# A two-layer decoder on one core: VectorE takes two of the four state rows of each step of the first scan's multiply by C

## The reference, cut to what matters

```python
def step(h, inp):
    dt_t, B_t, C_t, x_t = inp
    dA = jnp.exp(dt_t[:, :, None] * A[None])
    h = dA * h + (dt_t * x_t)[:, :, None] * B_t[:, None, :]
    y = jnp.einsum('bdn,bn->bd', h, C_t)
    return (h, y)
```

## Time and profile before

| | us |
|---|---|
| median of 3 runs | 3955.61 (3954.16 to 3958.93) |
| the profiled execution | 3953.2 |
| its span | 3951.4 |
| first scan, first decays to last sum (from the trace) | about 98 to 438 |
| VectorE busy over the span | 3177.0 (80%) |
| TensorE busy over the span | 3507.1 (89%) |
| GpSimd busy over the span | 1339.6 (34%) |

### The profile page before, as it was taken

The page is one execution under the profiler, slowest core; times in us unless marked ns, Lnnn a source line. Parts: engine busy times, 40 slices in busy tenths (PEclk is TensorE's granted clock), DMA queues, the critical chain, the costliest instruction groups (busy, mean ns, idle before and its releaser), DMA issues. The chain is left out here.

```text
span 3951.4 us, 41155 instructions
## 1 busy us (share of the span) xinstructions
PE 3507.1 (89%) x15310; PEld 1468.3 (37%) x15310; DVE 3177.0 (80%) x2733; ACT 1607.1 (41%) x2189; POOL 1339.6 (34%) x493
## 2 busy tenths in 40 slices
PE   5777779998999979998999989988999989976998
PEld 1222243334333443334333443334333443323444
DVE  5999569787999869887999869897999869895333
ACT  5666343214655353214655343214655343212001
POOL 3454304352344304352344304352344304351000
PEclk9788899989899999989899989999999989987999
DMA  6678402122233402122233302122233302110322
GB/s 230 244 277 299 172 15 74 58 74 71 88 106 97 136 22 72 60 72 72 88 105 98 131 27 72 57 75 72 88 105 98 133 25 72 58 45 11 104 96 72
DMA packets 105429, 382.92 MB, mean 97 GB/s; under 512 B 14224, under 2 KB 27920, under 8 KB 102800
## 3 DMA queue, kind: packets, MB, share of 16 engines
q1 hardware_dynamic: 85792, 346.50, 25.5%
q10 hardware_dynamic: 19440, 33.79, 3.1%
HBM read 290.80 MB, written 64.32 MB: 90 GB/s over the span
## 5 line engine op out<-in xcount | busy, mean ns | idle before, releaser
L300 PE MATMUL ps<-r,ring 128*128 128x512 bf16 (+1 forms) x2040 | 782.6, 384 | 0.0
L297 PE MATMUL ps<-xr,ring 128*128 128x512 bf16 x1568 | 613.1, 391 | 0.3 <-PEq L1822 0.3
L301 PE MATMUL ps<-xr,ring 128*128 128x512 bf16 x1568 | 610.6, 389 | 0.0
L297 PE MATMUL ps<-r,ring 128*128 128x512 bf16 (+3 forms) x1384 | 547.8, 397 | 55.2 <-DVE xc L1107 17.8
L301 PE MATMUL ps<-r,ring 128*128 128x512 bf16 (+3 forms) x1384 | 546.9, 396 | 0.0
L1159 POOL TENSOR_TENSOR hh<-hh,bc 128x2048 f32<-128x2048 f32 x72 | 334.7, 4649 | 520.9 <-DVE hh L1069 520.9
L1159 POOL TENSOR_TENSOR bc<-bc 128x2048 f32<-128x2048 f32 x64 | 304.2, 4752 | 344.7 <-DVE bc L1069 344.7
L1159 POOL TENSOR_TENSOR r<-r,bc 128x2048 f32<-128x2048 f32 x56 | 260.9, 4659 | 298.5 <-DVE r L1069 298.5
L1069 DVE TENSOR_TENSOR_SCAN hh<-da,hh 128x2048 f32<-128x2048 f32 x72 | 325.6, 4522 | 1.2
L1110 DVE TENSOR_TENSOR xc<-xc,ps 128x512 f32<-128x512 f32 x176 | 119.3, 678 | 225.0 <-PE ps L301 225.0
L1069 DVE TENSOR_TENSOR_SCAN bc<-da,bc 128x2048 f32<-128x2048 f32 x64 | 296.1, 4627 | 0.5
(11 more groups left out here) (269 smaller groups left out, 6519.5 us busy)
## 6 DMA issues: line engine op xcount, KB each, us to landing
ring<-wsplit SPq DMA_DIRECT2D x216, 768.0 KB, 4.2
r<-wstream SPq DMA_DIRECT2D x54, 768.0 KB, 6.9
ring<-wsplit SPq DMA_DIRECT2D x76, 512.0 KB, 4.0
wsplit<-ring SPq DMA_DIRECT2D x38, 768.0 KB, 4.5
da<-r ACTq DMA_DIRECT2D x360, 63.9 KB, 2.0
wsplit<-r SPq DMA_DIRECT2D x14, 768.0 KB, 4.6
r<-wstream SPq DMA_DIRECT2D x19, 512.0 KB, 6.2
r<-xT SPq DMA_DIRECT2D x7, 1024.0 KB, 6.3
```

The costliest lines, as they stand in the source:

```text
L297: mm = pe.matmul(out, w_hi, x_hi, start=start, stop=False)
L300: pe.matmul(out, w_hi, x_lo, start=False, stop=False)
L301: return pe.matmul(out, w_lo, x_hi, start=False, stop=stop)
```

## The change

In a call without feed-forward tiles (`halved`), GpSimd multiplies rows 0 and 1 of each quartet, and VectorE rows 2 and 3, right after `inputs(step+1)`. VectorE's part tells a new semaphore `own_read`, and `reduce_quad` waits for both. All other calls keep their instructions.

```diff
+        own_read, halved = sem("own_read"), not tiles
...
             def reduce_quad(j):
                 pe.wait_ge(read, 4 * j + 4)
+                if halved:
+                    pe.wait_ge(own_read, 4 * j + 4)
...
                 if step + 1 < blocks:
                     inputs(step + 1)
+                if halved and step < blocks:
+                    dve.wait_ge(scanned, step + 1)
+                    own = quartet(step)[:, GRP // 2:GRP, :]
+                    dve.tensor_tensor(own, own, k.out_rows[:, GRP // 2:GRP, :], ALU.mult).then_inc(own_read, 1)
                 if LAG <= step < pieces + LAG:
                     take_down(step - LAG)
...
             for s in range(blocks):
                 pool.wait_ge(scanned, s + 1)
-                pool.tensor_tensor(quartet(s), quartet(s), k.out_rows, ALU.mult).then_inc(read, 1)
+                rows = slice(0, GRP // 2 if halved else GRP)
+                pool.tensor_tensor(quartet(s)[:, rows, :], quartet(s)[:, rows, :], k.out_rows[:, rows, :], ALU.mult).then_inc(read, 1)
```

## The result

| | kernel before | changed kernel |
|---|---|---|
| median us (7 runs each) | 3957.98 | 3945.04 (3942.21 to 3951.57) |
| ratio, 95% interval | | 0.997 (0.9959 to 0.9981) |
| profiled execution, its span | 3953.2, 3951.4 | 3942.21, 3940.4 |
| start of the last sum's take-out in the first scan | 437.42 | 426.19 |

The changed kernel is 0.3% faster, 12.9 us by the medians; forecast were 9.9 us and 3945.7. The level lies closer to the forecast than the gain does because the median of the kernel before is 3957.98 over seven runs, where it was 3955.61 over the first three: that is luck. Of the 11.0 us between the two spans, the first scan holds 11.2; what follows it takes 3514.0 us before and 3514.2 after.

A forecast was written before the change was run, and what follows sets the result against it. VectorE taking turns with GpSimd, beside a loop of TensorE, ScalarE and weight loads, was taken as the bound. The walk's 8.7 us plus 1.2 at the end gave 9.9, from median 3955.6 to 3945.7; range 3932 to 3956.

The forecast's parts named there:

- The turns: First scan: VectorE and GpSimd alternate whole instructions when both operands are in SBUF; GpSimd's turn falls from 4.5 to 2.24 us.
- rival "slower": First scan: no turn shrinks and each own half adds 1.14 us in some 24 steps; 27 us slower, 3983; chance 0.08.
- The step sums: Steps set by VectorE: 8.88 to 7.9 us without a low part, 10.3 to 9.3 with one; gain 0.35 with `finish_y`.
- The rule of the Trainium skill: Elementwise work belongs on VectorE; by it alone each step gains 2.24 less 1.14 us, some 35 us in all.
- The walk: Through the first scan, counting gains that reach places where TensorE or ScalarE waits for VectorE; sum 9.9 us.
- the second and third stretch: First scan to 206.66, then to 256.29: TensorE idles and follows VectorE; gain reaches 3.0, then 6.3 us.
- the first stretch: First scan, start to 188.96: TensorE's and ScalarE's own chain fixes `inputs` twice; gain 0.
- the whole gain arrives: First scan: step gains and saved lost turns arrive if TensorE's chain also gets faster; 18 to 28 us, 3932; chance 0.14.
- the loop: First scan: a second loop of TensorE, ScalarE and weight loads beside VectorE's; where it sets the step, shorter VectorE steps gain nothing.
- Taken back by the loop: First scan: TensorE, ScalarE and weight loads bind also in steps given to VectorE; 0 to 6 us gain, 3952; chance 0.21.

The follow-up runs named there:

- the added work without the shorter turn: Against the kernel before: GpSimd still multiplies all four rows, and VectorE does an extra 128x1024 multiply on other data into an unused tile; 3987.28 us, ratio 1.0079.
- the run with the half first: Against the changed kernel: VectorE's half moved from behind `inputs` to right behind the scan, ahead of the low part; 3968.01 us, 23 us slower.
- the short rests: Float32 matmul of each weight rest left out, in both kernels: 3946.46 us on the kernel before, 3914.79 on the changed kernel; the pair differs by 31.7.

## Why the prediction was right

**The turns.** Right in both directions: all scans at 4.4 us, line 1066 at 0.68, and the added work without the shorter turn 31.6 us slower. The rival "slower" rested on turns that don't shrink. GpSimd's half took 2.35 us and not 2.24, which lets it end 0.1 later; VectorE's half pays for it with 0.2 us in steps without a low part.

**The step sums.** 7.86 us for 7.9; 9.32 for 9.3 (135.74 to 145.06 in the changed kernel's trace); 8.51 for 8.5 with `finish_y` (232.22 to 240.73). `finish_y` is uncovered, as argued.

**The rule of the Trainium skill** (GPSIMD Engine Reference, Performance versus the Vector engine) that elementwise work belongs on VectorE would have given 35 us here, and by the same rule all four rows should be better still. The runs say 12.9 for two rows and 5.9 slower for four, against the kernel before: what counts here is how long the two engines' turns are together, and what else VectorE has to do beside GpSimd's. What the trace showed of the turns (6.60 us for a scan of 4.41, 5.97 for a GpSimd multiply of 4.52) agrees with the Trainium skill, SBUF — State Buffer, Who interferes with whom: an exclusive lock for a whole instruction. That the waiting engine gets the turn ahead of the holder's next instruction is from the run with the half first (3.90 us at 303.60).

**The walk.** The gains at the places where the path passes between the engines, from starts in the two traces:

| place in the kernel before | forecast | measured |
|---|---|---|
| `inputs` after 188.96 | 0 | 3.5 |
| spread, 206.66 | 3.0 | 6.5 |
| spread, 256.29 | 6.3 | 9.8 |
| `inputs`, 285.75 | 6.3 | 8.1 |
| `inputs`, 349.28 | 8.3 | 9.7 |
| scan behind line 1063, 384.46 | 8.7 | 11.4 |
| last take-out, 437.42 | 9.9 | 11.2 |

In the second and third stretch 3.0 and 3.3 us were gained, as forecast, and behind the last scan 1.1 for 1.2. The other stretches were off, in both directions. In the first stretch I had TensorE's chain run through from the start and gave it nothing, but the spread at 134.78 had idled 1.89 us for line 1063, and the rests behind it now start at 134.06 and not at 135.84: 1.8 us. The remaining 1.7 are matmuls that ran less long at TensorE's lower clock (pairs of 1.91 and 1.46 us from 148.84 before, 1.37 and 1.02 after; of 1.91 and 1.42 from 179.64 before, 1.83 and 1.02 after). The same thing went the other way from 256.29 to 285.75, where I kept the gain at 6.3 and 1.6 us were lost. The rests of the changed kernel there:

```profile
250.72 1.91 PE L228 MATMUL ps<-r,squares_sb 128*128 128x512 f32 x2
252.85 1.37 PE L228 MATMUL ps<-r,squares_sb 128*128 128x512 f32 x2
...
266.08 1.58 PE L228 MATMUL ps<-r,squares_sb 128*128 128x512 f32 x2
```

and those of the kernel before:

```profile
260.59 1.26 PE L228 MATMUL ps<-r,squares_sb 128*128 128x512 f32 x2
261.90 1.02 PE L228 MATMUL ps<-r,squares_sb 128*128 128x512 f32 x2
...
274.76 1.02 PE L228 MATMUL ps<-r,squares_sb 128*128 128x512 f32 x2
```

A pair takes 1.02 us where the granted clock is 1.00 of full speed (2.4 GHz; 271.0 to 272.5 in the changed kernel) and 1.91 to 2.08 where it is 0.50 (1.2 GHz; 248.5 to 252.5). TensorE had idled 1.99 us ahead of this stretch in the changed kernel (4.30 before), so shorter idling did not bring a higher clock, against what I put down for the rival "the whole gain arrives". What sets the moment of the rise stays open.

From 349.28 to 384.46 the gain grew by 1.7 for 0.4: in the kernel before, ScalarE's high part of 357.12 had waited 1.40 us for its load, and in the changed kernel there is no such wait there.

```profile
357.12 1.48 ACT L260 ACTIVATE ring<-r 128x1536 bf16<-128x1536 f32 x1 [1.40 <-DMA r<-wstream]
```

Behind 384.46 I let TensorE follow VectorE with its whole gain. It had idled only 2.37 us there; in the changed kernel its own chain sets that spread (374.52 for 384.68, a gain of 10.2), and `inputs` at 411.94 gains 10.2, not the 11.4 reached before.

So the 9.9 came near the 11.2 partly by luck. The terms that I had too small (3.5 in the first stretch, 1.3 by the late load) and too large (1.6 by the clock, 0.4 on the way to 349.28, 1.4 at the end) nearly cancel.

**The rivals.** "The whole gain arrives" (18 to 28 us) is refuted for this kernel; that the loop holds it back is confirmed by the short rests, where 31.7 us arrive. "Taken back by the loop" was the right mechanism at a smaller size: VectorE's waits for TensorE and ScalarE rose from 17.1 to 31.2 us, where I had looked for 20 or more in `inputs` alone; that part came to 18.9, and the late low parts took the 12.3.

## What to carry to other kernels

A busy share can hold waiting. Where VectorE's operation with two operands in SBUF is longer than elsewhere, look for GpSimd beside it, and count the pair as one queue; dividing GpSimd's work paid here, where VectorE has an operation without such a need (an operand in PSUM) to run beside it. Then walk the path through the places where another engine idles for the sped-up one: what is gained arrives there, at most as far as that engine had idled, and what is queued behind a wait adds to the path. Expect such a walk to be off by a us or two in a stretch, as here by TensorE's clock and a late load. Before an operation is moved up a list, look at what follows it: a partner that waits gets the turn first.

## What the runs showed of the hardware that I had not expected

The turn goes to the waiting engine between two instructions of the holder: the low part right behind VectorE's half took 3.90 us for 1.73 with GpSimd waiting since 302.50. A half of GpSimd's multiply costs 2.35 us against 4.52 for the whole, so I estimate about 0.2 us per instruction as fixed; the quarter of the run with three rows on VectorE, 1.27 us, fits.
